# Writing the built adjacency blocks contiguously in PSUM and reordering them in ScalarE's copy

## What is computed

```python
def _mp_layer(x, src, dst, edge_attr, W, b):
    src2, dst2 = src + self loops, dst + self loops
    msg = concatenate([x[dst2], x[src2], ea2], axis=1) @ W + b
    agg = segment_sum(msg, dst2, num_segments=n)
    return relu(agg)

h   = _mp_layer(x, src, dst, edge_attr, W1, b1)
h   = relu(h)
out = _mp_layer(h, src, dst, edge_attr, W2, b2)
x   = layernorm(x + log_softmax(out, axis=1))
```

## Time and profile before

| what | value |
|---|---|
| median of three executions | 245.91 us (245.29 to 246.37) |
| the profiled execution | 245.42 us |
| its span in the profile | 243.6 us |
| TensorE busy | 203.7 us, 2092 matmuls |
| VectorE busy | 179.0 us |
| GpSimd busy | 148.1 us |
| ScalarE busy | 118.6 us |
| window matmuls L849 | 600, 59.0 us busy |
| ScalarE's copies of a set, L762 | 75, 77.5 us busy |

### The profile page before, as it was taken

One profiled execution on the slowest core, in us unless ns is written; L12 is line 12 of the kernel. 1 busy time (PEld: TensorE's weight loads), 2 busy tenths in 40 slices (PEclk: granted clock), 3 DMA queues, 4 the chain that ended last, 5 costly groups with the idle time before them and its releaser, 6 DMA issues.

```text
span 243.6 us, 5581 instructions
## 1 busy us (share of the span) xinstructions
PE 203.7 (84%) x2092; PEld 182.0 (75%) x2092; DVE 179.0 (73%) x459; ACT 118.6 (49%) x242; POOL 148.1 (61%) x334
## 2 busy tenths in 40 slices
PE   0423498999989999899998999989999999999940
PEld 0113497888768798778987789878889999999930
DVE  2968989887876978889788897777201193998982
ACT  2406466667557677576775767757720010111110
POOL 6549351899977999978999689999674000000000
PEclk9999999999979999999999999999999999999995
DMA  1340100000000000000000000000000001011000
GB/s 40 110 125 0 44 0 3 1 14 2 13 0 13 0 5 0 3 0 4 1 3 0 3 0 6 0 3 1 0 3 3 0 3 32 3 32 25 18 16 17
DMA packets 8908, 3.31 MB, mean 14 GB/s; under 512 B 8091, under 2 KB 8406, under 8 KB 8881
## 3 DMA queue, kind: packets, MB, share of 16 engines
q1 hardware_dynamic: 7841, 1.98, 4.0%
q0 software_dynamic: 1040, 0.97, 1.6%
HBM read 2.13 MB, written 0.81 MB: 12 GB/s over the span
## 4 chain that ended last, share of the span: by engine, by line
PE 40%; POOL 27%; DVE 19%; DMA 6%; issue 4%; ACT 1%; DVEq 0%; POOLq 0%; ACTq 0%
PE pset L882 21%; PE acc L874 9%; DVE ohr L530 5%; PE pset L849 5%; DVE ohl L530 5%; POOL u L381 4%; POOL deg L380 3%; POOL u L384 3%; DMA x_nat<-in_x_tiles 2%; POOL t L399 2%; DMA adj<-in_edges,adj 2%; POOL adj L324 2%; POOL zr L397 2%; POOL t L395 2%; DVE s_sum L561 2%
## 5 line engine op out<-in xcount | busy, mean ns | idle before, releaser
L762 ACT ACTIVATE adj<-pset 125x1000 bf16<-125x1000 f32 x75 | 77.5, 1033 | 10.7 <-PE pset L849 10.7
L874 PE MATMUL acc<-x,adj 125*125 125x195 bf16 x625 | 74.2, 256 | 1.5 <-DVE s_sum L561 1.4
L530 DVE TENSOR_TENSOR ohl<-iota,keys 128x1000 bf16<-128x1000 bf16 (+1 forms) x75 | 56.8, 758 | 15.3 <-PE dense L862 13.9
L849 PE MATMUL pset<-ohr,ohl 128*125 128x125 bf16 x600 | 59.0, 252 | 9.0 <-DVE ohr L530 8.9
L874 PEld LDWEIGHTS acc<-x,adj 125*125 125x125 bf16 x625 | 58.2, 140 | 5.3 <-issue 1.8
L849 PEld LDWEIGHTS pset<-ohr,ohl 128*125 128x125 bf16 x600 | 50.0, 152 | 11.0 <-DVE ohr L530 6.7
L530 DVE TENSOR_TENSOR ohr<-iota,keys 128x1000 bf16<-128x1000 bf16 (+1 forms) x75 | 57.2, 762 | 0.0
L882 PE MATMUL pset<-z,adj 125*125 125x192 bf16 x625 | 52.8, 246 | 0.0
L882 PEld LDWEIGHTS pset<-z,adj 125*125 125x125 bf16 x625 | 51.7, 136 | 0.3
L380 POOL TENSOR_SCALAR deg<-s_sum 125x1 f32<-125x1 f32 x25 | 12.4, 497 | 18.5 <-DVE s_sum L561 18.5
L561 DVE TENSOR_REDUCE s_sum<-acc 125x65 f32<-125x195 f32 x25 | 9.0, 360 | 17.7 <-PE acc L874 16.3
(11 more groups left out here) (118 smaller groups left out, 255.0 us busy)
## 6 DMA issues: line engine op xcount, KB each, us to landing
x_nat<-in_x_tiles SPq DMA_DIRECT2D x1, 406.2 KB
x_nat<-in_x_tiles SPq DMA_DIRECT2D x1, 375.0 KB
out<-x SPq DMA_DIRECT2D x2, 187.5 KB
out<-x SPq DMA_DIRECT2D x3, 93.8 KB
adj<-in_dst SPq DMA_DIRECT2D x1, 208.5 KB
out<-x SPq DMA_DIRECT2D x1, 125.0 KB
adj<-in_edges,adj POOLq DMA_INDIRECT x5, 4.6
adj<-in_edge_attr,adj POOLq DMA_INDIRECT x5, 3.5
```

Source lines behind the costliest of these rows:

```text
L530: ins = dve.tensor_tensor(out=oh[s][:, :, :, :], in0=iota2[:, 0:Q, :].unsqueeze(1).broadcast_to([128, n, Q, 2]), in1=key[:, g, k0:k0 + 2 * ...
L762: act.activation(adj4[0:Q, g, :, w0:w0 + 8 * WD].rearrange("p h (b e) -> p b h e", b=2), pset[s][0:Q, :, 0:4 * WD * G].rearrange("p b (h e ...
L849: ins = pe.matmul(pset[s][0:Q, i // 4, 0:4 * WD * G].rearrange("p (h e) -> p h e", h=G)[:, :, i % 4 * WD:(i % 4 + 1) * WD], ohl[s][:, i // ...
L874: ins = pe.matmul(acc[0:Q, 0:XW], adj4[0:Q, g, h, :], x3[:, h, :], start=(h == 0), stop=(h == G - 1))
```

## The change

Two places change. The window matmul i of a set writes its 125 columns side by side, in the order in which it makes them (h outer, e inner), into columns 128 (i mod 4) to 128 (i mod 4) + 124 of its bank. Before, it wrote 25 runs of 5 columns, 20 columns apart, so that the four matmuls of a bank interleaved into the 500 columns (h, window, e).

ScalarE's copy of a set moves the same 1000 numbers per partition. Before, it went bank by bank, read 500 columns side by side in each, and wrote 50 runs of 20 elements into `adj`. Now it goes block by block (h), then window (w), then e: it reads 200 runs of 5 columns, 128 columns apart within a block, and writes 25 runs of 40 elements.

```diff
@@ -759,8 +759,9 @@
                 else:
                     w0 = SETS[s][0] * WD
-                    act.activation(adj4[0:Q, g, :, w0:w0 + 8 * WD].rearrange("p h (b e) -> p b h e", b=2),
-                                   pset[s][0:Q, :, 0:4 * WD * G].rearrange("p b (h e) -> p b h e", h=G), ACT.Copy)\
+                    act.activation(adj4[0:Q, g, :, w0:w0 + 8 * WD].rearrange("p h (w e) -> p h w e", e=WD),
+                                   pset[s][0:Q, :, :].rearrange("p b (w c) -> p (b w) c", c=128)[:, :, 0:WD * G]
+                                   .rearrange("p w (h e) -> p h w e", h=G), ACT.Copy)\
                        .then_inc(evac[s], 1)
@@ -847,7 +848,7 @@
                 for i in range(8):
                     ins = pe.matmul(
-                        pset[s][0:Q, i // 4, 0:4 * WD * G].rearrange("p (h e) -> p h e", h=G)[:, :, i % 4 * WD:(i % 4 + 1) * WD],
+                        pset[s][0:Q, i // 4, i % 4 * 128:i % 4 * 128 + WD * G],
                         ohl[s][:, i // 2, :, i % 2], ohr[s][:, i // 2, :, i % 2], start=True, stop=True)
                 ins.then_inc(built[s], 1)
```

## The result

The changed kernel takes 247.42 us (median of ten runs, 246.54 to 248.49), the kernel before 245.72 in ten runs beside it. The ratio is 1.0064, with a 95% interval of 1.0043 to 1.0086: slower, by about 1.7 us, where 1.5 us less were forecast. It also lies just outside the stated range.

A forecast was written before the change was run, and what follows sets the result against it. TensorE, busy 84%, was taken to set the pace where nothing stalls, GpSimd or VectorE in other groups. 1.7 us from the chain less 0.2 gave a 1.5 us gain: 244.4 us from 245.91, range 242.6 to 247.0.

The forecast's parts named there:

- The matmul: Window matmuls on TensorE: spacing falls from 70 to 60 ns, saving 80 ns a build, 6.0 us over all 600.
- rival 2: Window matmuls: 70 ns spacing belongs to weight loads or strided one-hots, only 22 ns a build go; 245.7 us; chance 0.12.
- The copy: ScalarE's copy of a set: bounds 1017 and 1301 ns, 1033 ns taken, no change.
- Rival 3: ScalarE's copy: at the high end each takes 268 ns more and ScalarE slows the kernel to 249.4 us; chance 0.13.
- The share on the chain: Window matmuls on the chain that sets the end: 5% of the span, 12.2 us, of which 1.7 us go.
- The 0.2 us "for the places where it does not" stay ahead: GpSimd in groups where it does not stay ahead of faster builds: 0.2 us taken off the gain.
- The gain of 1.7 us: Window matmuls on the chain: 10 of 70 ns of their 12.2 us saved, before 0.2 us is taken off.
- The 0.25 us of room for GpSimd: Group without stalls: 5.46 us less GpSimd's busy 5.21; three faster builds take 240 ns, so it just stays ahead.
- Rival 1: GpSimd's chain takes over in more places and hides the gain, leaving 0 to 1.2 us: 244.7 to 245.9 us; chance 0.21.
- The clock, rival 4: TensorE's three other waits for `zs` lengthen and bring its clock to half: 248.3 us if all three do; chance 0.07.

The follow-up runs named there:

- set 2 alone: Kernel before, with the new layout and copy only for set 2, built behind the single window; sets 0 and 1 as before: 246.20 us, ratio 1.0044.

## Why the prediction was wrong

- **The matmul.** Right: spacing of 60 ns forecast, 61 measured; a build 0.66 us forecast, 0.65 measured; the median 221 and 222 ns. The change does what it says, and rival 2 is out.
- **The copy.** Right in size: bounds of 1017 and 1301 ns with 1033 chosen, 1013 measured, 4 below the low bound. The high end came from L757's 1.5 ns for a written run laid on the reads. The window-by-window copy shows that this is the price of the written side (200 of them: 1336 ns). Rival 3 is out.
- **The share on the chain.** The step that failed. "5% of 243.6 us are 12.2 us, and 10 of 70 ns of it are 1.7 us (...) The rest, 4.3 us, becomes a longer wait of TensorE" held GpSimd's operations at the lengths of the old trace. They are not lengths of their own: the cast is 0.18 us long in a pause of VectorE and 0.78 us behind the start of a one-hot, and L384 is 0.29 or 0.89 us. The 0.2 us "for the places where it does not" stay ahead were a guess at this. In its place stand two collisions in each five groups, 0.56 and 0.51 us by the windows, against 0.37 us that the other three groups give back: 0.70 us a cycle on 30.49 in the middle of the kernel, 0.2 in its first cycle. In the profiled execution the two groups around the longer half clock are another 1.3 us longer. The gain of 1.7 us itself shows nowhere: where VectorE's wait takes the collisions away, the faster builds measure 0.2 us, within the noise, because TensorE waits longer for `zs`. The 0.25 us of room for GpSimd was misread in the same way. Busy time counts also the time for which an operation is held up: in the group without a stall GpSimd was busy for 5.21 us before and is for 4.54 us now (5.30 us long).
- **Rival 1** had the place, GpSimd's chain, and the reason, that "its operations vary with what VectorE does beside it". It stopped the loss at the gain, as if a hidden saving were the worst that could come, and gave no price to a pause of 0.20 us with a single window that comes 0.15 us sooner. The trace of before held what it needed: VectorE idle for a fraction of a microsecond ahead of its wide one-hot, and one operation of GpSimd at two lengths, here least, median and most:

```profile
L384 POOL TENSOR_TENSOR u<-x_nat,deg x25: 284/291/898, 36.4 to 181.4; 125x64 f32<-125x64 f32 x25
```

- **The clock, rival 4.** The longer stretch is in the profiled execution (mean clock 0.973), but the two executions of the changed kernel with a mean clock of 0.987 took 246.5 and 246.9 us, while ten executions of the kernel before at that same clock took 244.2 to 245.2. So it is not what makes the kernel slower. The three later waits for `zs` did not grow (1.01, 1.01 and 0.93 us against 1.08, 1.06 and 0.95), and they brought no half clock. GpSimd's lateness was taken up by the waits for `u` ahead of them: with the wait for u on VectorE they are 1.30 to 1.38 us.

What stays open: why set 2 alone costs 0.4% and the copy's order alone 0.2%, where the cycles of their profiles show neither; the 0.8 us between the profiled execution of the set-2 kernel and its median; and how much of the change's loss the second place (`base` and L384) has by itself. The window-by-window copy has the first place without the second, but with a slower copy, and no other run parts them.

## What to carry to other kernels

When an engine gets faster, ask what it releases. If VectorE waited for it, its pauses may be the only time in which GpSimd runs, and the length of GpSimd's operations in the trace holds only for those pauses: look for the same operation at two lengths (here 0.29 and 0.88 us for L384, before anything was changed), and for an idle time of VectorE shorter than the saving. A chain of waits says where a saving can count, not that the rest is free; a short wait put on purpose (VectorE for GpSimd's cast) can be worth more than the saving: here it gave back the loss of 0.6%, and the saving gave nothing.

## What the runs showed of the hardware

- A matmul that writes 25 runs of 5 fp32 columns into PSUM costs about 9 ns more in spacing (70 to 61) and 21 ns more from start to end than one that writes 125 columns side by side.
- ScalarE reads 200 runs of 5 fp32 from PSUM as fast as 50 runs of 20 (1013 ns for 1000 columns, each with 25 written runs of 40), but with 200 written runs of 5 bf16 the copy takes 1336 ns: 323 ns for 175 written runs more, 1.8 ns a run.
- The same GpSimd operation is short while VectorE is idle and long behind the start of a one-hot: the cast of 125 x 3 numbers 0.18 and 0.78 us, L384 0.29 and 0.89 us.
- 75 matmuls more with their weight loads, in a program of 2092, put 1.2 to 1.7 us outside the profiled span, whose length is near that of the kernel before (243.4 to 244.9 us in nine executions, 243.6 in the profiled one of before). What they are the profile does not show.
